# Linear attention of a five-stage kernel: the masked logits become the stationary operand, and the attended values leave TensorE in rows

## The chip, the cores and the metric

The kernel runs on one core of one Trainium2 chip. The metric is the device time of one execution in microseconds, the median of three runs. TensorE (PE in the profile) does the matmuls and transposes, VectorE (DVE), ScalarE (ACT) and GpSimd (POOL) the rest, and SyncE's queue (SP) starts most DMAs. The engines run side by side and wait for one another by semaphores.

## The reference

The program is a small Perceiver of two blocks on x of shape (16, 64, 512): cross-attention, gated attention and a quantised linear layer, then cross-attention, linear attention and a mixture of eight experts, each added to x. The change lies in the second linear attention and at the seam to the mixture behind it. What is computed there:

```
x5  = layernorm(x)                                   # 16 items of 64 rows, 512 features
q   = softmax(x5 @ Wq.T + bq, over features)
k   = softmax(x5 @ Wk.T + bk, over the 64 rows) / sqrt(512)
v   = softmax(x5 @ Wv.T + bv, over the 64 rows)
x   = x + (q @ k.T) @ v                              # item by item
x6  = layernorm(x)
x   = x + sum over experts of gate_e * (relu(x6 @ wi.T + bi + (x6 @ A_e.T) @ B_e.T) @ wo.T + bo)
```

## The kernel before, in words

All 1024 rows of x stand in SBUF as `X[128, 8, 512]`: 8 tiles of 128 rows. A tile holds two items of 64 rows, a "pair", so pair j is tile j. Each stage has one instruction stream for each engine, written out by hand in Python loops; the order of the work is the order of the code, and nothing is scheduled later.

`l1_linear_attention` first projects keys and values into feature-major form (`kT`, `vT`), makes the softmax over rows there, and turns `vT` back into rows `V[:, j, :]`. Then a loop over rounds t works on all pairs, a pair in several steps, each step one or two rounds after the one before:

- `queries_pe(t)`: 12 matmuls for the queries of pair t (TensorE, printed as L288, since all products go through one helper).
- DVE subtracts the minimum (L2312), ACT makes the exponential (L2392), DVE takes the reciprocal and scales (L2322, L2323).
- `turn_queries_pe(t-1)`: 4 transposes (L2187); ACT copies them to `qT` (L2388).
- `attended_pe(t-2)`: 4 products of 128x128, stationary the values of the pair, moving the masked logits `at` (L2208). The result is feature-major, so it has to be turned back.
- `logits_pe(t-1)`: 4 products summed in bank 3 (L2196); DVE multiplies with the block mask into `at` (L2318), so that the two items of a pair don't see each other.
- ACT copies the attended values to `oT` (L2398), `back_pe_of(t-3)` turns them into rows by 4 transposes (L2216), and DVE adds them to `X` (L2327, in the next stage L2687). Behind the sum come the statistics of the next layernorm (L219 to L221), the power on GpSimd (L225) and the normalisation (L229).

An fp32 product of 128x128 appears in the trace as two matmul records, so the 32 products of L2208 are 64 records there; a transpose is one record.

The eight pairs take the rounds t = 0 to 10. On DVE the sums of pairs 6 and 7 stand at the start of the next stage, `l1_mixture`. There TensorE turns the eight normalised tiles (L235: tiles 0 to 3 from the last rounds of the stage before, tiles 4 to 7 behind the first split `xT` of `rows_v`, L305), turns the matrices of LoRA (L2591, L2602, L2604), and makes the gate's logits: 24 products with 8 columns stationary (L288, `gwT`). After that the stage runs over 16 blocks of the hidden layer. `load_half` brings the first two pieces of `wi` into `XT`, where `V` stands until then.

Of the kernel before, what the change touches and what calls it, by code (L numbers as in the profile page):

```python
# [9 lines left out]
ALU = mybir.AluOpType  # L10
# [3 lines left out]
P = 128  # L14
NI, NP, D = 16, 64, 512
NK = 512
C = D // P
KT = NK // P
ROWS = NI * NP
G = ROWS // P  # L20
# [48 lines left out]
def build(nc, a, out):  # L69
# [12 lines left out]
    with ctx:  # L82
# [126 lines left out]
        av = signal("av")  # L209
        back_pe = signal("back_pe")  # L210

# [1852 lines left out]
        def l1_linear_attention():  # L2064
# [7 lines left out]
            o4 = W[:, 0, 1, :].rearrange("p (c n) -> p c n", c=C)  # L2072
            oT = W[:, 5, 0:2, :]
            low = kept["low5"]
# [20 lines left out]
            lg_v = signal("e_lg_v")  # L2095
            at_pe = signal("e_at_pe")
            at_a = signal("e_at_a")

# [7 lines left out]
            def gpsimd():  # L2106
                row_stats_pool(4, PAIRS - 1)
                pool.wait_ge(av.s, av(0))
                p(pool.memset(block[:], 0.0))
                for h in range(2):  # L2110
                    ins = pool.memset(block[h * NP:(h + 1) * NP, h * NP:(h + 1) * NP], 1.0)
                    if h == 0:
                        p(ins)
                ins.then_inc(setup_pool.s, 1)
                pool.wait_ge(setup_pool.s, setup_pool(0))
                for k in range(len(units)):
                    pool.wait_ge(inv_v.s, inv_v(k))
                    seg = segments(k)
                    pool.tensor_tensor(seg, seg, ext[:, k, :].unsqueeze(2).broadcast_to([P, NI // 2, NP]), ALU.mult).then_inc(soft.s, 1)
                for j in range(PAIRS - 2):  # L2120
                    row_stats_pool(5, j)
# [78 lines left out]
            def attended_pe(j):  # L2200
                pe.wait_ge(lg_v.s, lg_v(j))
                pe.wait_ge(vrow_a.s, vrow_a(j if j >= 4 else 3))
                if j >= 2:
                    pe.wait_ge(at_a.s, at_a(j - 2))
                elif j == 0:
                    pe.wait_ge(vrow_a.s, vrow_a(PAIRS - 1))
                for c in range(C):
                    ins = pe.matmul(bank[:, 4 + j % 2, c * P:(c + 1) * P], V[:, j, c * P:(c + 1) * P], at[:], start=True, stop=True)  # L2208
                ins.then_inc(at_pe.s, 1)

            def back_pe_of(j):
                pe.wait_ge(at_a.s, at_a(j))
                if j >= 2:
                    pe.wait_ge(xsum.s, xsum(4 * G + j - 2))
                for c in range(C):
                    ins = pe.transpose(bank[:, 6 + j % 2, c * P:(c + 1) * P], oT[:, j % 2, c * P:(c + 1) * P], ident[:])  # L2216
                ins.then_inc(back_pe.s, 1)

            def tensor():
# [16 lines left out]
                for j in range(4, PAIRS):  # L2236
                    value_rows_pe(j)
                for t in range(1, PAIRS + 3):
                    if t < PAIRS:
                        queries_pe(t)  # L2240
                    if t <= PAIRS:
                        turn_queries_pe(t - 1)
                    if 2 <= t <= PAIRS + 1:
                        attended_pe(t - 2)
                    if t == PAIRS + 1:
                        for g in range(4):
                            transpose_rows(xn6, 5, g, g)
                    if t <= PAIRS:
                        logits_pe(t - 1)
                    if 3 <= t:  # L2250
                        back_pe_of(t - 3)

# [28 lines left out]
            def vector():  # L2281
# [23 lines left out]
                dve.wait_ge(setup_pool.s, setup_pool(0))  # L2305
                for t in range(PAIRS + 3):
                    if t < PAIRS:
# [6 lines left out]
                    if 1 <= t <= PAIRS:  # L2314
                        dve.wait_ge(lg_pe.s, lg_pe(t - 1))
                        if t >= 2:
                            dve.wait_ge(at_pe.s, at_pe(t - 2))
                        dve.tensor_tensor(at[:], bank[:, 3, 0:P], block[:], ALU.mult).then_inc(lg_v.s, 1)  # L2318
                    if t < PAIRS:
# [3 lines left out]
                        dve.tensor_scalar(qj, qj, total, None, ALU.mult).then_inc(probs.s, 1)  # L2323
                    if 3 <= t < PAIRS + 1:
                        j = t - 3
                        dve.wait_ge(back_pe.s, back_pe(j))
                        dve.tensor_tensor(X[:, j, :], X[:, j, :], bank[:, 6 + j % 2, :], ALU.add).then_inc(xsum.s, 1)  # L2327
                        if j:
                            normalise(xn6, 5, j - 1)
                        dve.wait_ge(xsum.s, xsum(4 * G + j))  # L2330
                        row_stats_v(j)
                normalise(xn6, 5, PAIRS - 3)

# [25 lines left out]
            def scalar():  # L2359
# [21 lines left out]
                for j in range(4, PAIRS):  # L2381
                    value_rows_a(j)
                for t in range(PAIRS + 2):
                    if 1 <= t <= PAIRS:
# [4 lines left out]
                    if t < PAIRS:  # L2389
                        qj, lo, total = q[:, t % 2, :], low[:, t % 2, 0:1], low[:, t % 2, 1:2]  # L2390
                        act.wait_ge(lowest.s, lowest(t))
                        act.activation(qj, qj, ACT.Exp, bias=lo, scale=-1.0, accum_out=total).then_inc(expd.s, 1)  # L2392
                    if t >= 2:
                        j = t - 2
                        act.wait_ge(at_pe.s, at_pe(j))
                        if j >= 2:
                            act.wait_ge(back_pe.s, back_pe(j - 2))
                        act.copy(oT[:, j % 2, :], bank[:, 4 + j % 2, :]).then_inc(at_a.s, 1)  # L2398

# [12 lines left out]
        def l1_mixture():  # L2412
# [77 lines left out]
            def sync():  # L2490

                sp.wait_ge(turned.s, turned(5 * G))
                load_half(0)
                load_half(1)
                for q in range(2, 2 * FT // 4):
# [3 lines left out]
            def gpsimd():  # L2499
                pool.wait_ge(score.s, score(PAIRS - 1))  # L2500
                pool.iota(rank[:], pattern=[[-1, E]], base=E, channel_multiplier=0,
                          allow_small_or_imprecise_dtypes=True).then_inc(setup_pool.s, 1)
                for j in (PAIRS - 2, PAIRS - 1):
                    row_stats_pool(5, j)
                pool.wait_ge(setup_pool.s, setup_pool(0))
# [93 lines left out]
            def tensor():  # L2599
                pe.wait_ge(small_in.s, small_in(1))  # L2600
                for c in range(C):
                    ins = pe.transpose(bank[:, 4, c * E:(c + 1) * E], small[0:E, 1, c * P:(c + 1) * P], ident[0:E, 0:E])  # L2602
# [81 lines left out]
            def vector():  # L2684
                for j in (PAIRS - 2, PAIRS - 1):
                    dve.wait_ge(back_pe.s, back_pe(j))
                    dve.tensor_tensor(X[:, j, :], X[:, j, :], bank[:, 6 + j % 2, :], ALU.add).then_inc(xsum.s, 1)  # L2687
                for j in (PAIRS - 2, PAIRS - 1):
                    dve.wait_ge(xsum.s, xsum(4 * G + j))
                    row_stats_v(j)  # L2690
                for g in range(4):
                    rows_v(g)
                dve.wait_ge(wt_a.s, wt_a(0))
                split_v(gwT[:, 1, :, :], gw_src, gwT[:, 0, :, :]).then_inc(wt_v.s, 1)
                for j in (PAIRS - 2, PAIRS - 1):
                    normalise(xn, 5, j)
                for g in range(4, G):
# [210 lines left out]
```

## Time and profile before

| | |
|---|---|
| median of 3 runs | 1278.16 us (1274.45 to 1279.21) |
| profiled execution | 1274.7 us, its span 1273.4 us |
| PE busy | 1222.2 us, 96% of the span |
| DVE, ACT, POOL busy | 730.6, 521.3, 141.2 us |
| chain that ended last | PE 84%, DVE 9%, ACT 4% |
| granted TensorE clock, mean | 0.988 of full speed |
| rounds of the changed stage and the seam | about 965 to 1025 us of the span |

Matmuls are pipelined: a row of the timeline gives the time from the first start to the last (modelled) end, and the next instruction can begin before that end. The chain cuts these overlaps away.

### The profile page before, as it was taken

How to read it: one execution, taken by the hardware profiler on the slowest of the kernel's cores; microseconds unless marked ns; L12 is line 12 of the kernel's file. 1: busy time of each engine (PE TensorE's matmuls, PEld its weight loads, DVE VectorE, ACT ScalarE, POOL GpSimd, SP SyncE). 2: the span in 40 equal slices, each digit the busy share in tenths (PEclk: the TensorE clock that was granted, in tenths of full speed). 3: DMA queues.
4: the chain of work that ended last, by engine and by line, in shares of the span. 5: the costliest groups of instructions: out<-in, count | busy, mean ns of one | idle time of the engine just before them, and what ended most of it. 6: DMA issues, size and time to landing. Idle time of an engine off the chain costs nothing.

```text
span 1273.4 us, 25892 instructions
## 1 busy us (share of the span) xinstructions
PE 1222.2 (96%) x11069; PEld 914.6 (72%) x11069; DVE 730.6 (57%) x1604; ACT 521.3 (41%) x1033; POOL 141.2 (11%) x163
## 2 busy tenths in 40 slices
PE   6999989999979999999999999999899999999999
PEld 4664477865537777777777777777788868888887
DVE  4458386749894555454555555555685756344442
ACT  3234356653122354544454545454454432222321
POOL 2300012055642000000000000000031100000000
PEclk9999999899999999999999999999999899999999
DMA  9659700100204020100010000000400201110100
GB/s 296 249 199 394 286 2 1 66 9 1 99 18 165 1 100 35 34 35 34 35 35 35 35 34 35 34 35 34 85 1 1 75 1 34 33 34 33 66 34 33
DMA packets 49334, 88.23 MB, mean 69 GB/s; under 512 B 19210, under 2 KB 20284, under 8 KB 45124
## 3 DMA queue, kind: packets, MB, share of 16 engines
q1 hardware_dynamic: 48160, 86.01, 19.4%
q8 instruction: 88, 1.44, 0.4%
q10 hardware_dynamic: 1060, 0.56, 0.2%
q14 instruction: 26, 0.21, 0.1%
HBM read 65.59 MB, written 20.97 MB: 68 GB/s over the span
## 4 chain that ended last, share of the span: by engine, by line
PE 84%; DVE 9%; ACT 4%; DMA 1%; issue 1%; POOL 1%; SPq 0%; POOLq 0%; DVEq 0%; ACTq 0%
PE bank L288 58%; PE bank L245 4%; PE bank L1762 3%; PE bank L564 2%; PE bank L1783 2%; PE bank L546 2%; PE bank L1111 1%; PE bank L1132 1%; DVE W L1360 1%; PE bank L235 1%; PE bank L2527 1%; PE bank L491 1%; DVE stats L219 1%; DMA W<-ctx_turned 1%; PE bank L2196 1%
## 5 line engine op out<-in xcount | busy, mean ns | idle before, releaser
L1995 ACT ACTIVATE W<-W,low 128x512 f32<-128x512 f32 x128 | 91.0, 713 | 57.2 <-DVE low L1901 57.2
L1975 ACT ACTIVATE K<-bank,vecT 128x512 f32<-128x512 f32 x64 | 43.8, 689 | 166.2 <-PE bank L288 166.2
L225 POOL TENSOR_TENSOR rstd<-rstd,half_pow 128x1 f32<-128x1 f32 x48 | 31.6, 660 | 697.7 <-DVE rstd L221 697.7
L1874 DVE TENSOR_TENSOR W<-bank,vecT 128x256 f32<-128x256 f32 x16 | 6.8, 424 | 163.6 <-PE bank L1783 163.6
L1901 DVE CUSTOM_DVE_ANT_0 W<-bank,W 128x512 f32<-128x512 f32 x128 | 80.8, 687 | 30.5 <-PE bank L1762 30.5
L288 PE MATMUL bank<-ctxT,Wkv 128*128 128x512 f32 x384 | 93.6, 396 | 0.3 <-DVE ctxT L305 0.3
L288 PE MATMUL bank<-xT,wT 128*128 128x512 f32 x384 | 92.7, 391 | 0.8 <-ACT W L2829 0.5
L288 PE MATMUL bank<-Wq,Wkv 128*128 128x512 f32 x384 | 93.0, 394 | 0.0
L288 PE MATMUL bank<-Wkv,ctxT 128*128 128x512 f32 x384 | 92.9, 394 | 0.0
L288 PE MATMUL bank<-Wkv,Wq 128*128 128x512 f32 x384 | 92.1, 395 | 0.0
L288 PE MATMUL bank<-woT,hR 128*128 128x512 f32 x384 | 91.7, 394 | 0.1
L288 PEld LDWEIGHTS bank<-Wkv,ctxT 128*128 128x128 f32 x384 | 70.8, 188 | 27.1 <-issue 13.0
L288 PEld LDWEIGHTS bank<-Wkv,Wq 128*128 128x128 f32 x384 | 70.8, 188 | 27.2 <-issue 13.0
L288 PEld LDWEIGHTS bank<-xT,wT 128*128 128x128 f32 x384 | 71.8, 188 | 17.3 <-issue 1.3
L288 PEld LDWEIGHTS bank<-ctxT,Wkv 128*128 128x128 f32 x384 | 70.8, 188 | 15.9 <-issue 1.2
L288 PEld LDWEIGHTS bank<-woT,hR 128*128 128x128 f32 x384 | 70.9, 188 | 14.8 <-DVE W_late L2755 0.5
L288 PEld LDWEIGHTS bank<-Wq,Wkv 128*128 128x128 f32 x384 | 70.9, 188 | 14.8
L2002 ACT COPY PT<-bank 128x512 f32<-128x512 f32 x128 | 65.7, 600 | 19.4 <-PE bank L245 19.4
L1909 DVE TENSOR_SCALAR W<-W,total 128x512 f32<-128x512 f32 x128 | 62.3, 487 | 4.6
L2844 ACT ACTIVATE h<-bank,vecT 128x512 f32<-128x512 f32 x32 | 22.1, 690 | 95.2 <-PE bank L288 90.9
L245 PEld LDWEIGHTS bank<-ident,W 32*128 32x128 f32 x2752 | 46.3, 137 | 19.2 <-issue 11.9
L288 PE MATMUL bank<-z,BT 128*128 128x512 f32 x192 | 53.0, 400 | 0.1
(347 smaller groups left out, 2233.1 us busy)
## 6 DMA issues: line engine op xcount, KB each, us to landing
W<-ctx_turned SPq DMA_DIRECT2D x16, 1024.0 KB, 4.7
W<-in_ctx_dram SPq DMA_DIRECT2D x8, 1024.0 KB, 11.0
ctx_turned<-ctxT SPq DMA_DIRECT2D x8, 1024.0 KB, 8.0
ctx_turned<-W SPq DMA_DIRECT2D x8, 1024.0 KB, 6.8
XT<-in_ctx_dram SPq DMA_DIRECT2D x4, 1024.0 KB, 11.3
XT<-in_L_ffn_wi_dram SPq DMA_DIRECT2D x4, 1024.0 KB, 6.3
XT<-in_L_ffn_wo_dram SPq DMA_DIRECT2D x4, 1024.0 KB, 5.0
raw_own<-in_ctx_dram SPq DMA_DIRECT2D x3, 1024.0 KB, 10.8
```

Of the source, the lines that this page charges most:

```text
L225: pool.tensor_tensor(rstd[:, g:g + 1], rstd[:, g:g + 1], half_pow[:], ALU.pow).then_inc(rstd_ok.s, 1)
L245: ins = pe.transpose(bank[:, first + r, to:to + 32], src_of(t, k)[strip, :], ident[strip, strip])
L288: ins = pe.matmul(dst, stationary(x, k), moving(y, k), start=(first and n == 0), stop=(last and n == len(passes) - 1), skip_group_check=True)
L546: ins = pe.matmul(bank[b * NP:(b + 1) * NP, 4, :], q2T[:, c, j * P + b * NP:j * P + (b + 1) * NP], ctxT[j % 2][:, b, c, :], start=(c == 0) ...
L564: ins = pe.matmul(bank[b * NP:(b + 1) * NP, 6, :], pT[:, k, b * NP:(b + 1) * NP], raws[j % 4][:, b, k, :], start=(k == 0), stop=(k == KT - 1))
L1762: ins = pe.matmul(bank[s2 * NP:(s2 + 1) * NP, 4 + r, :], qT[strip, 2 * rnd + s2, i * NP:(i + 1) * NP], K[strip, 2 * rnd + s2, :], start=Tr ...
L1783: ins = pe.matmul(b[32 * r:32 * r + 32, c * NP:(c + 1) * NP], V[:, k, c * P + 32 * r:c * P + 32 * r + 32], PT[:, 4 * (c // 2) + r, k, NP * ...
L1901: dve.tensor_tensor_reduce(out=PR[:, j, :], in0=bank[:, 4 + j % 4, :], in1=mask, scale=1.0, scalar=3.0e38, op0=ALU.add, op1=ALU.min, accum ...
L1909: dve.tensor_scalar(PR[:, j, :], PR[:, j, :], total[:, j:j + 1], None, ALU.mult).then_inc(probs.s, 1)
L1975: act.activation(K[:, m, :], bank[:, n % 4, :], ACT.Identity, bias=pcol("L1_xattn_bk", m)).then_inc(ring_a.s, 1)
L1995: act.activation(PR[:, j, :], PR[:, j, :], ACT.Exp, bias=low[:, j:j + 1], scale=-1.0, accum_out=total[:, j:j + 1]).then_inc(expd.s, 1)
L2002: act.copy(PT[:, 4 * half:4 * half + 4, :, strip].rearrange("p t k n -> p (t k) n"), bank[:, 4 + n % 4, :].rearrange("p (a n) -> p a n", n ...
```

## The change

The product is formed the other way round: `at` (the masked logits, 128x128) is stationary, the values `V[:, j, :]` (128x512) move, and the result of one matmul call is already in rows. The transposes back, ACT's copy to `oT` and their semaphores go. Four banks (4 to 7) are used in turn for the result, instead of two and two. DVE adds pair t-2 in round t (before: t-3), so that the loop has one or two rounds fewer on each engine. At the seam, three of the four transposes of normalised tiles come before the last attended product, only pair 7's sum is left to the next stage on DVE, and the normalisation of pair 6 comes before the statistics of pair 7. The second piece of `wi` now waits for the last attended product, since it lands where `V` is read.

```diff
             def attended_pe(j):
                 pe.wait_ge(lg_v.s, lg_v(j))
                 pe.wait_ge(vrow_a.s, vrow_a(j if j >= 4 else 3))
-                if j >= 2:
-                    pe.wait_ge(at_a.s, at_a(j - 2))
+                if j >= 4:
+                    pe.wait_ge(xsum.s, xsum(4 * G + j - 4))
                 elif j == 0:
                     pe.wait_ge(vrow_a.s, vrow_a(PAIRS - 1))
-                for c in range(C):
-                    ins = pe.matmul(bank[:, 4 + j % 2, c * P:(c + 1) * P], V[:, j, c * P:(c + 1) * P], at[:], start=True, stop=True)
-                ins.then_inc(at_pe.s, 1)
-
-            def back_pe_of(j):
-                pe.wait_ge(at_a.s, at_a(j))
-                if j >= 2:
-                    pe.wait_ge(xsum.s, xsum(4 * G + j - 2))
-                for c in range(C):
-                    ins = pe.transpose(bank[:, 6 + j % 2, c * P:(c + 1) * P], oT[:, j % 2, c * P:(c + 1) * P], ident[:])
-                ins.then_inc(back_pe.s, 1)
+                pe.matmul(bank[:, 4 + j % 4, :], at[:], V[:, j, :], start=True, stop=True).then_inc(rows_out.s, 1)
...
-                for t in range(1, PAIRS + 3):
+                for t in range(1, PAIRS + 2):
                     if t < PAIRS:
                         queries_pe(t)
                     if t <= PAIRS:
                         turn_queries_pe(t - 1)
+                    if t == PAIRS + 1:
+                        for g in range(3):
+                            transpose_rows(xn6, 5, g, g)
                     if 2 <= t <= PAIRS + 1:
                         attended_pe(t - 2)
                     if t == PAIRS + 1:
-                        for g in range(4):
-                            transpose_rows(xn6, 5, g, g)
+                        transpose_rows(xn6, 5, 3, 3)
                     if t <= PAIRS:
                         logits_pe(t - 1)
-                    if 3 <= t:
-                        back_pe_of(t - 3)
...
-                for t in range(PAIRS + 3):
+                for t in range(PAIRS + 1):
...
-                    if 3 <= t < PAIRS + 1:
-                        j = t - 3
-                        dve.wait_ge(back_pe.s, back_pe(j))
-                        dve.tensor_tensor(X[:, j, :], X[:, j, :], bank[:, 6 + j % 2, :], ALU.add).then_inc(xsum.s, 1)
+                    if 2 <= t:
+                        j = t - 2
+                        dve.wait_ge(rows_out.s, rows_out(j))
+                        dve.tensor_tensor(X[:, j, :], X[:, j, :], bank[:, 4 + j % 4, :], ALU.add).then_inc(xsum.s, 1)
                         if j:
                             normalise(xn6, 5, j - 1)
                         dve.wait_ge(xsum.s, xsum(4 * G + j))
                         row_stats_v(j)
-                normalise(xn6, 5, PAIRS - 3)
...
-                    if t >= 2:
-                        j = t - 2
-                        act.wait_ge(at_pe.s, at_pe(j))
-                        if j >= 2:
-                            act.wait_ge(back_pe.s, back_pe(j - 2))
-                        act.copy(oT[:, j % 2, :], bank[:, 4 + j % 2, :]).then_inc(at_a.s, 1)
...
                 load_half(0)
+                sp.wait_ge(rows_out.s, rows_out(PAIRS - 1))
                 load_half(1)
...
             def vector():
-                for j in (PAIRS - 2, PAIRS - 1):
-                    dve.wait_ge(back_pe.s, back_pe(j))
-                    dve.tensor_tensor(X[:, j, :], X[:, j, :], bank[:, 6 + j % 2, :], ALU.add).then_inc(xsum.s, 1)
-                for j in (PAIRS - 2, PAIRS - 1):
-                    dve.wait_ge(xsum.s, xsum(4 * G + j))
-                    row_stats_v(j)
+                dve.wait_ge(rows_out.s, rows_out(PAIRS - 1))
+                dve.tensor_tensor(X[:, PAIRS - 1, :], X[:, PAIRS - 1, :], bank[:, 4 + (PAIRS - 1) % 4, :],
+                                  ALU.add).then_inc(xsum.s, 1)
+                normalise(xn, 5, PAIRS - 2)
+                dve.wait_ge(xsum.s, xsum(4 * G + PAIRS - 1))
+                row_stats_v(PAIRS - 1)
                 for g in range(4):
                     rows_v(g)
...
-                for j in (PAIRS - 2, PAIRS - 1):
-                    normalise(xn, 5, j)
+                normalise(xn, 5, PAIRS - 1)
```

First TensorE in one round, where the names after the arrow are the moving and the stationary operand. Before:

```order
L288 MATMUL bank<-Wkv,xT 128x512 x12
L2187 MATMUL bank<-ident,q 128x128 x4
L2208 MATMUL bank<-at,XT 128x128 x4
L2196 MATMUL bank<-qT,W 128x128 x4
L2216 MATMUL bank<-ident,W 128x128 x4
```

And after (the lines of the file have moved; L2184 is the old L2187, L2204 the attended product, L2193 the logits):

```order
L288 MATMUL bank<-Wkv,xT 128x512 x12
L2184 MATMUL bank<-ident,q 128x128 x4
L2204 MATMUL bank<-XT,at 128x512
L2193 MATMUL bank<-qT,W 128x128 x4
L288 MATMUL bank<-Wkv,xT 128x512 x12
```

The four transposes behind the logits are gone, and the next queries follow the logits at once.

TensorE at the seam, from the last logits on, as a difference (`W` with `ident` are the normalised tiles and the matrices of LoRA):

```order
-L2216 MATMUL bank<-ident,W 128x128 x4
-L2208 MATMUL bank<-at,XT 128x128 x4
-L235 MATMUL bank<-ident,W 128x128 x16
-L2216 MATMUL bank<-ident,W 128x128 x8
-L2602 MATMUL bank<-ident,W 128x8 x4
-L2604 MATMUL bank<-ident,W 128x128 x4
...
+L235 MATMUL bank<-ident,W 128x128 x12
+L2204 MATMUL bank<-XT,at 128x512
+L235 MATMUL bank<-ident,W 128x128 x4
+L2583 MATMUL bank<-ident,W 128x8 x4
+L2585 MATMUL bank<-ident,W 128x128 x4
```

Twelve transposes back (of pairs 5, 6 and 7) are gone, and the last attended product moved behind twelve of the sixteen tile transposes.

DVE from the last masked logits to the first split of the seam. Before:

```order
L2318 TENSOR_TENSOR at5<-bank,block5 128x128 [waits e_at_pe,e_lg_pe]
L2327 TENSOR_TENSOR X<-X,bank 128x512 [waits back_pe]
L229 TENSOR_SCALAR W<-X,mv,rstd 128x512 [waits rstd_ok]
L219 BN_STATS stats<-X 128x6 [waits xsum]
...
L229 TENSOR_SCALAR W<-X,mv,rstd 128x512 [waits rstd_ok]
L2687 TENSOR_TENSOR X<-X,bank 128x512 [waits back_pe] x2
L219 BN_STATS stats<-X 128x6 [waits xsum]
...
L219 BN_STATS stats<-X 128x6 [waits xsum]
...
L305 TENSOR_TENSOR xT6<-bank,xT6 128x4x128 [waits xt_a] x4
```

And after:

```order
L2305 TENSOR_TENSOR at5<-bank,block5 128x128 [waits rows_out,e_lg_pe]
L2314 TENSOR_TENSOR X<-X,bank 128x512 [waits rows_out]
L229 TENSOR_SCALAR W<-X,mv,rstd 128x512 [waits rstd_ok]
L219 BN_STATS stats<-X 128x6 [waits xsum]
...
L2667 TENSOR_TENSOR X<-X,bank 128x512 [waits rows_out]
L229 TENSOR_SCALAR W<-X,mv,rstd 128x512 [waits rstd_ok]
L219 BN_STATS stats<-X 128x6 [waits xsum]
...
L305 TENSOR_TENSOR xT6<-bank,xT6 128x4x128 [waits xt_a] x4
```

Between the last `at` and the first `xT6` DVE had three sums, three sets of statistics and two normalisations; now it has two of each.

## Rows read from the trace of the kernel before

**Rows 1.** The page's first part: busy time and share of each engine.
```profile
PE 1222.2 (96%) x11069; PEld 914.6 (72%) x11069; DVE 730.6 (57%) x1604; ACT 521.3 (41%) x1033; POOL 141.2 (11%) x163
```
**Rows 2.** Waits, 965 to 1025: waiting for releaser, total us, times, longest.
```profile
DVE at L2318 <- PE bank L2196: 11.5, 8, 1.6
DVE q L2312 <- PE bank L288: 5.7, 7, 1.9
```
**Rows 3.** Chain of waits through the rounds: start us, us, what.
```profile
969.96 2.76 PE bank L288 x12
...
974.99 2.77 PE bank L288 x12
...
980.04 0.44 PE bank L2216 x4
...
1001.90 0.02 issue
```
**Rows 4.** Timeline of two rounds: start, us, engine, line, tiles, [idle before].
```profile
967.53 0.60 PE L2187 MATMUL bank<-ident,q 128*128 128x128 f32 x4
...
968.80 1.16 PE L2196 MATMUL bank<-qT,W 128*128 128x128 f32 x8 [0.68 <-ACT qT L2388]
...
985.55 0.29 DVE L2318 TENSOR_TENSOR at<-bank,block 128x128 f32<-128x128 f32 x1 [1.57 <-PE bank L2196]
...
988.34 0.15 DVE L221 TENSOR_SCALAR rstd<-mv 128x1 f32<-128x1 f32 x1
988.53 0.60 PE L2187 MATMUL bank<-ident,q 128*128 128x128 f32 x4
...
988.73 0.69 DVE L2312 CUSTOM_DVE_ANT_0 q<-bank,bq 128x512 f32<-128x512 f32 x1 [0.23 <-PE bank L288]
...
989.17 0.59 ACT L2388 COPY qT<-bank 128x512 f32<-128x512 f32 x1 [3.67 <-PE bank L2187]
...
989.86 1.10 PE L2196 MATMUL bank<-qT,W 128*128 128x128 f32 x8
```
**Rows 5.** Timeline: one attended product that waited for its input (8 records).
```profile
1005.74 1.16 PE L2208 MATMUL bank<-at,XT 128*128 128x128 f32 x8
```
**Rows 6.** Timeline at 267.61: the same shape as the new product.
```profile
267.61 1.12 PE L1088 MATMUL bank<-oT,centring 128*128 128x512 f32 x2
```
**Rows 7.** That source line: durations of one record, ns, min/median/max.
```profile
L1088 PE MATMUL bank<-oT,centring x16: 592/645/697, 267.6 to 337.9; 128*128 128x512 f32 x16
```
**Rows 8.** Chain of waits at the seam.
```profile
1002.87 0.66 PE bank L2187 x4
...
1005.35 0.45 PE bank L2216 x4
...
1013.07 1.97 PE bank L235 x8
...
1024.36 0.02 issue
```
**Rows 9.** Timeline of DVE at the seam.
```profile
1005.83 0.69 DVE L2327 TENSOR_TENSOR X<-X,bank 128x512 f32<-128x512 f32 x1
...
1007.83 0.15 DVE L221 TENSOR_SCALAR rstd<-mv 128x1 f32<-128x1 f32 x1
...
1008.64 0.55 DVE L229 TENSOR_SCALAR W<-X,mv,rstd 128x512 f32<-128x512 f32 x1 [0.66 <-POOL rstd L225]
...
1011.33 0.68 DVE L219 BATCH_NORM_STATS2 stats<-X 128x6 f32<-128x512 f32 x1
...
1012.33 2.47 DVE L305 TENSOR_TENSOR xT<-bank,xT 128x512 fp32r<-128x512 f32 x4
```
**Rows 10.** Stretches at the seam: length, busy us of each engine, granted clock, DMA share, GB/s.
```profile
1005.35:1010.45 5.10, 5.09 (x45) 4.48 (x42) 4.18 (x10) 2.64 (x5) 0.80 (x3) 1.00 0.36 44
1010.45:1013.07 2.62, 0.00 (x1) 0.01 (x1) 2.48 (x8) 0.67 (x2) 1.13 (x3) 0.84 1.01 300
1013.07:1018.10 5.03, 5.03 (x24) 5.03 (x25) 3.94 (x8) 2.81 (x5) 1.36 (x5) 0.50 0.69 269
1018.10:1024.36 6.26, 6.26 (x28) 2.52 (x27) 3.17 (x5) 1.00 (x3) 0.00 (x0) 0.92 0.01 3
```

More of the change, by code:

```diff
@@ L209, in build @@
         av = signal("av")
-        back_pe = signal("back_pe")
+        rows_out = signal("rows_out")
         side_by_side = {}
@@ L2072, in l1_linear_attention @@
             o4 = W[:, 0, 1, :].rearrange("p (c n) -> p c n", c=C)
-            oT = W[:, 5, 0:2, :]
             low = kept["low5"]
@@ L2095, in l1_linear_attention @@
             lg_v = signal("e_lg_v")
-            at_pe = signal("e_at_pe")
-            at_a = signal("e_at_a")
             def sync():
@@ L2119, in gpsimd @@
                     pool.tensor_tensor(seg, seg, ext[:, k, :].unsqueeze(2).broadcast_to([P, NI // 2, NP]), ALU.mult).then_inc(soft.s, 1)
-                for j in range(PAIRS - 2):
+                for j in range(PAIRS - 1):
                     row_stats_pool(5, j)
@@ L2316, in vector @@
                         if t >= 2:
-                            dve.wait_ge(at_pe.s, at_pe(t - 2))
+                            dve.wait_ge(rows_out.s, rows_out(t - 2))
                         dve.tensor_tensor(at[:], bank[:, 3, 0:P], block[:], ALU.mult).then_inc(lg_v.s, 1)
@@ L2382, in scalar @@
                     value_rows_a(j)
-                for t in range(PAIRS + 2):
+                for t in range(PAIRS + 1):
                     if 1 <= t <= PAIRS:
@@ L2502, in gpsimd @@
                           allow_small_or_imprecise_dtypes=True).then_inc(setup_pool.s, 1)
-                for j in (PAIRS - 2, PAIRS - 1):
-                    row_stats_pool(5, j)
+                row_stats_pool(5, PAIRS - 1)
                 pool.wait_ge(setup_pool.s, setup_pool(0))
@@ L2600, in tensor @@
                 pe.wait_ge(small_in.s, small_in(1))
+                pe.wait_ge(xsum.s, xsum(4 * G + PAIRS - 3))
                 for c in range(C):
@@ L2694, in vector @@
                 split_v(gwT[:, 1, :, :], gw_src, gwT[:, 0, :, :]).then_inc(wt_v.s, 1)
-                for j in (PAIRS - 2, PAIRS - 1):
-                    normalise(xn, 5, j)
+                normalise(xn, 5, PAIRS - 1)
                 for g in range(4, G):
```

## Prediction

> **What bounds the kernel now.** I read the page's busy shares first: TensorE is busy for 96% of the span [rows 1], so time is won where TensorE's own work shortens, or where the few stretches in which it waits shorten. Second, the chain of waits through the rounds of the changed stage [rows 3]: from 974.99 on the chain is TensorE alone, piece after piece, and the four transposes back (L2216, 0.44 us) stand on it. Third, the waits of the same stretch [rows 2]: DVE waits for TensorE 11.5 us in all at `at` and 5.7 us at the query minimum. DVE follows, it does not lead. Fourth, the chain at the seam [rows 8] and DVE's timeline there [rows 9]: between 1005.35 and 1013.07 the chain leaves TensorE. The reader is to see that TensorE stands idle for the last 2.6 us of it [rows 10] until DVE has made two sums, two sets of statistics and the first split. Last, the granted clock in the stretches at the seam [rows 10]: it is down to 0.50, the 1.2 GHz level, from 1013.07 to 1018.10.
>
> **The rounds: the transposes back.** A round without them shows in the trace itself: from 969.96 to 974.99, 5.03 us, and from 974.99 to the end of the logits at 980.04, 5.05 us. From there to 1001.90 [rows 3] lie four rounds that each contain four transposes back: 21.86 us, 5.46 each. After the change they should take 5.04 each, since the queries that follow have their bank free. That is 4 x 0.42 = 1.7 us less. The transposes of pair 4 end beside a wait for DVE's scaled query (TensorE's next piece starts at 1002.87 [rows 8], 0.97 us after the logits), so they were hidden and give nothing. Those of pairs 5 to 7 belong to the seam.
>
> **The rounds: the attended product.** It stands between the transposes of the query (L2187) and the logits (L2196), and the logits need ACT's copy of those transposes. In a round with the product the logits start 1.33 us after the transposes (988.53 to 989.86, with the copy ending at 989.76); in the first round, which has no product, they start 1.27 us after (967.53 to 968.80), and there they take 1.16 us instead of 1.10, because nothing was before them to hide the first weight load [rows 4]. Both end 2.43 us after the transposes began. So the product costs nothing today: ACT's copy covers it, and if it becomes shorter nothing is won. The new form isn't in this stage's trace. The same shape elsewhere, two records of 128x512 fp32 behind a wait, took 1.12 us [rows 6]; the old form behind a wait took 1.16 us [rows 5]. That bounds it from below at -0.04. From above, if the two records did not overlap at all, it would be 2 x 0.70 us [rows 7], 0.24 us more than 1.16; in seven rounds and at the seam that is up to 1.9 us more. I take 0, since the row of the same shape is the nearest one.
>
> **The rounds: DVE.** The sum, normalisation and statistics are done by DVE one round sooner, which adds no work to a full round. But the round is shorter. From the masked logits (985.55) to the last statistic (988.49) DVE needs 2.94 us, and the next queries are ready 2.78 us after the logits once the transposes no longer stand between; before, DVE had 0.23 us left there (the wait before 988.73) [rows 4]. So the query minimum starts about 0.2 us late. It feeds ACT's exponential, which anyway stands behind ACT's own copy of `qT`, and the scaled query is not needed until the next round's transposes. DVE's load in a round is 2.94 + 0.69 = 3.6 us of 5.04. I take 0; if the 0.2 us passed through in the six rounds that have both queries and a sum, it would be 1.2 us. ACT's copy to `oT` goes, but ACT waits 3.67 us a round [rows 4], so that gives nothing.
>
> **Last round.** From 1001.90 to 1005.35 (3.45 us) nothing changes: TensorE waits for the scaled query, then transposes, product, logits. It starts 1.7 us sooner.
>
> **The seam up to the first split.** Counted from the end of the last logits (1005.35 before), TensorE's tiles 4 and 5 started at 7.72 us (1013.07) [rows 8]. After: DVE makes `at` (0.33), then sum, normalisation and statistics of pair 6, 2.15 us by the rows of pair 5 (1005.83 to 1007.98 [rows 9]), free at about 2.45. TensorE meanwhile does 12 tile transposes (3 x 0.44 = 1.3) and then the last product (1.1), so pair 7 is also ready at about 2.45: the two meet. Then pair 7's sum 0.69, the normalisation of pair 6 that waits for GpSimd's power (0.66 wait before, here hidden by the sum all but a few hundredths; 0.5), statistics 1.0 (1011.33 to 1012.33), and 0.74 from there to TensorE's start (1012.33 to 1013.07) [rows 8, 9]. The sum is 2.45 + 0.6 + 0.5 + 1.0 + 0.74 = 5.3 us instead of 7.7: 2.4 us less. If the last product took the upper bound, 0.2 of it would go. What could be late next are ACT's copies of tiles 0 to 3, but they begin 0.6 us after the last logits and four take 2.4 us. The weight pieces of `wi` start about 3 us and 1.5 us sooner than TensorE's old schedule; the first is used only behind the gate. The new wait on SP has only `load_half(1)` and later pieces behind it, and it ends 2.5 us after the last logits.
>
> **The seam's clock.** Before, from 1013.07 to 1018.10 TensorE did 24 transposes in 5.03 us at clock 0.50, and the gate's logits behind them ran 6.26 us at 0.92 [rows 10]. At the full clock 24 transposes are 6 x 0.44 = 2.6 us by [rows 3], and the logits 5.8, together 2.9 us less than the 11.3 that they took. TensorE had had no product other than transposes from 1006.9 on [rows 5] before the clock fell, and 2.6 us of idleness. After the change the same stretch is about 6 us instead of 11, with about 1.6 us idle. Whether the dip stays is not decided by any row: the bounds are 0 (it costs the same) and -2.9 (it is gone). I take -1.2, a dip that remains but in less work; the normalisation of pair 6, which the old order left until the first four splits were done, can no longer hold the transposes up.
>
> The Trainium skill ("TensorE: Matmul & The Clock Gate", Part 4: PE-mode transpose) says that transposes don't count as TensorE being busy for the clock. The trace agrees as far as it goes: TensorE was busy 5.03 of 5.03 us with transposes from 1013.07, and the clock stayed at 0.50 [rows 10]. By this rule the change, which puts 12 transposes in a row before the last product and leaves 36 behind it, could keep the dip and even start it sooner.
>
> **Sum.** -1.7 - 2.4 - 1.2 = -5.3 us on an execution of 1274.7 us (span 1273.4, and 1.3 us around it): 1269.4 us. Everything behind the gate's logits hangs on TensorE in the same way as before and just moves. The profiled execution is 3.5 us below the median of the three runs and near the lowest of them; against the median 1278.2 the forecast is 1272.8 us, 0.41% less. A change under 0.5% can hardly be told from none in this kernel, whose three runs lie 0.37% apart.
>
> **Rivals.**
> First, the clock dip goes entirely, as the stretch without products is halved. For it: the last logits and the last product now stand 2.5 us nearer to the gate's logits. Against it: most of that stretch is still transposes and idleness. Then -1.7 - 2.4 - 2.9 = -7.0 us, 1271.2 us.
> Second, what is won comes back: the dip costs as much as before (0) and DVE, which now has no slack at the query minimum, passes 0.2 us on in six rounds (+1.2). For it: 0.23 us of slack is less than the 0.42 us by which the round shortens [rows 4]. Against it: DVE waits 1.57 us for the logits in the same round [rows 4]. Then -1.7 - 2.4 + 1.2 = -2.9 us, 1275.3 us.
> Third, slower: the clock falls before the seam. TensorE's wait for the scaled query in the last round grows from 0.5 to 0.97 us, since the hidden transposes are gone, and the transposes of tiles then come before the last product. If the clock stood at 0.50 from there to the end of the gate's logits, all of TensorE's work in between would double: transposes, product and logits 2.4 us, 16 + 8 tile and LoRA transposes 2.6, the last product 0.9, 24 transposes 2.6 and the gate 5.8, together 14.3 us. Of the added 14.3 about 3 us fall into TensorE's waits. Against the rows of before, -4.1 - 2.9 + 14.3 - 3 = +4.3 us, 1282.5 us. It turns the sign once more than about 10 us (at full clock) of TensorE's work there are at the low level. Against it: from 1005.35 to 1010.45, with 36 transposes and one product, the clock was still 1.00 [rows 10].
>
> **Chances and range.** Forecast 0.55; dip gone 0.22; won and lost 0.16; slower 0.07 (and this one mostly by less than 0.5%). The likeliest case's own range is a gain of 3 to 6.4 us, 1271.8 to 1275.2; single executions spread over 5 us and a median of three by some 2 us either way, so I give 1267.5 to 1277.5. Faster by over 0.5% (6.4 us) is the second case and the edge of the first: 0.27. Within 0.5%: 0.69. Slower: 0.04.
>
> **What would show it.** Right: the chain's rounds of the changed stage 5.03 to 5.08 us; the attended product as two records in about 1.1 us behind the transposes, with the logits still 1.33 us after these; 3.4 us from there to the last logits; TensorE's L235 of tiles 4 and 5 at 5.2 to 5.4 us after the last logits; the gate's logits over 8.5 to 11 us after that. Wrong: rounds over 5.2 us, with a wait of TensorE on DVE or ACT before the transposes or the logits; the split at the seam waiting for ACT; a clock of 0.50 in the rounds themselves.

## The result, and the profile after

The changed kernel takes 1270.9 us (median of 18 executions, 1266.4 to 1277.3) against 1276.9 us of the kernel before (18 executions in the same comparison, 1270.3 to 1282.2). The ratio is 0.9955, with a 95% interval of 0.9941 to 0.9969: about 0.45% faster, and clear of noise. The forecast was 1272.8 us and 0.41%. One execution of the kernel before in a later comparison (1382.1 us) and one of e2 (1737.4 us) ran at a much lower granted clock (0.844 and 0.747) and are left out of all ratios and means below.

The page's first part, which answers to [rows 1]:

```profile
PE 1214.2 (96%) x10989; PEld 902.6 (71%) x10989; DVE 730.6 (58%) x1604; ACT 516.7 (41%) x1025; POOL 141.0 (11%) x163
```

ACT has lost its eight copies (1033 instructions before) and DVE kept all of its own. TensorE has 80 records fewer: 32 transposes back, and 8 products of two records in place of 32 with two.

The waits of the changed stage, against [rows 2]:

```profile
DVE at L2305 <- PE bank L2193: 10.9, 8, 1.6
DVE q L2299 <- PE bank L288: 2.6, 3, 1.9
```

DVE still waits for TensorE at the masked logits. At the query minimum it waited 7 times before and now 3 times: in the rounds that also have a sum, DVE has become the later one there.

The chain of waits through the rounds and over the seam, to set against [rows 3] and [rows 8]:

```profile
968.59 2.74 PE bank L288 x12
...
973.60 2.77 PE bank L288 x12
...
977.67 0.97 PE bank L2193 x8
978.64 2.74 PE bank L288 x12
...
998.75 0.02 issue
...
1002.21 0.02 issue
...
1002.53 0.59 DVE X L2314
...
1005.25 0.55 DVE W L229
...
1006.80 0.61 DVE xT L305
...
1007.46 1.25 PE bank L235 x8
...
1016.10 0.02 issue
```

From 978.64 the queries follow the logits at once. The four rounds to 998.75 take 20.11 us (21.86 before). Last logits to tiles 4 and 5: 1002.21 to 1007.46, 5.25 us (7.72). From there to the end of the gate's logits: 8.64 us (11.29). The stretches of the seam, against [rows 10] (length, busy us of PE, PEld, DVE, ACT, POOL, granted clock, DMA share, GB/s):

```profile
1005.73:1007.46 1.73, 0.01 (x1) 0.01 (x1) 1.66 (x6) 0.67 (x2) 0.57 (x2) 1.00 0.77 253
1007.46:1010.27 2.81, 2.81 (x24) 2.55 (x25) 2.81 (x7) 2.12 (x5) 1.36 (x5) 1.00 0.94 331
1010.27:1016.10 5.83, 5.83 (x29) 2.43 (x28) 3.66 (x7) 1.27 (x4) 0.00 (x0) 1.00 0.15 58
```

TensorE is idle for 1.7 us instead of 2.6, and in this execution the clock does not fall: the 24 transposes take 2.8 us, not 5.0.

One round on its engines, against [rows 4]:

```profile
981.22 0.60 PE L2184 MATMUL bank<-ident,q 128*128 128x128 f32 x4
...
981.59 0.69 DVE L2299 CUSTOM_DVE_ANT_0 q<-bank,bq 128x512 f32<-128x512 f32 x1
...
981.65 1.02 PE L2204 MATMUL bank<-XT,at 128*128 128x512 f32 x2
...
981.85 0.59 ACT L2374 COPY qT<-bank 128x512 f32<-128x512 f32 x1 [3.71 <-PE bank L2184]
...
982.49 0.97 PEld L2193 LDWEIGHTS bank<-qT,W 128*128 128x128 f32 x8 [0.64 <-ACT qT L2374]
982.51 1.14 PE L2193 MATMUL bank<-qT,W 128*128 128x128 f32 x8
```

The weight loads (PEld) of the logits wait 0.64 us for ACT's copy, and the product's two records fill just that time. DVE's minimum has no idle time in front of it.

The two profiled executions differ by 8.2 us of span (1273.4 and 1265.2), which is more than the change gives. 1.4 us of it lie before the first full round (969.96 against 968.59), where both kernels have the same instructions. The rest: rounds 1.75 us, the seam up to tiles 4 and 5 2.47 us, and the stretch from there to the end of the gate's logits 2.65 us, here called the clock's part.

### The profile page after: what moved, and what is told of

Same layout as the page of the kernel before. It is cut to its first block, busy times and chain, and to the rows that moved or that the text cites. A ratio compares the mean times of both kernels' runs of the same rounds, so it can differ in the third digit from the quotient of the medians.

```text
span 1265.2 us, 25713 instructions
## 1 busy us (share of the span) xinstructions
PE 1214.2 (96%) x10989; PEld 902.6 (71%) x10989; DVE 730.6 (58%) x1604; ACT 516.7 (41%) x1025; POOL 141.0 (11%) x163
## 4 chain that ended last, share of the span: by engine, by line
PE 84%; DVE 9%; ACT 4%; issue 1%; DMA 1%; POOL 1%; SPq 0%; POOLq 0%; DVEq 0%; ACTq 0%
PE bank L288 58%; PE bank L245 4%; PE bank L1762 3%; PE bank L1783 2%; PE bank L564 2%; PE bank L546 2%; PE bank L1111 1%; PE bank L1132 1%; DVE W L1360 1%; PE bank L2507 1%; PE bank L235 1%; PE bank L491 1%; DVE stats L219 1%; DMA W<-ctx_turned 1%; PE bank L2193 1%
```

## The experiments

Spans and means below are of executions of each kernel; the kernel before ran in every comparison. Its 44 executions in the comparisons of e1 to e7 have a mean of 1277.3 us, the 23 of the changed kernel (the result and e7) 1270.7 us.

**e1_sums_late.** The new product, with DVE's sums and the seam in the old order (TensorE's tile transposes stand behind the last product again, too):

```diff
-                    if 2 <= t:
-                        j = t - 2
+                    if 3 <= t:
+                        j = t - 3
...
             def vector():
-                dve.wait_ge(rows_out.s, rows_out(PAIRS - 1))
-                dve.tensor_tensor(X[:, PAIRS - 1, :], X[:, PAIRS - 1, :], bank[:, 4 + (PAIRS - 1) % 4, :],
-                                  ALU.add).then_inc(xsum.s, 1)
-                normalise(xn, 5, PAIRS - 2)
-                dve.wait_ge(xsum.s, xsum(4 * G + PAIRS - 1))
-                row_stats_v(PAIRS - 1)
+                for j in (PAIRS - 2, PAIRS - 1):
+                    dve.wait_ge(rows_out.s, rows_out(j))
+                    dve.tensor_tensor(X[:, j, :], X[:, j, :], bank[:, 4 + j % 4, :], ALU.add).then_inc(xsum.s, 1)
+                for j in (PAIRS - 2, PAIRS - 1):
+                    dve.wait_ge(xsum.s, xsum(4 * G + j))
+                    row_stats_v(j)
```

> The changed kernel with the sums and the seam in the old order: DVE adds pair t-3 in round t, the sums of pairs 6 and 7 and both their statistics stand at the start of the next stage, and the four tile transposes come behind the last product. The new product form stays, without transposes back. Theory A (rounds and seam are separate terms): rounds stay at 5.03 to 5.05 us, and tiles 4 and 5 (L235 x8) start 7.4 to 7.6 us after the last logits instead of 5.25, so 2.2 us of the gain go. If the clock dip at the seam comes back with the longer stretch without products, another 1 to 2.7 us go. Rival B (the shorter rounds only work because DVE's sums come sooner, or the reverse): rounds over 5.2 us.

Measured: ratio to the kernel before 0.9985 (0.9966 to 1.0004), so in whole executions it is not told from the kernel before. Chain at the seam (DVE's sums of the last two pairs, then TensorE):

```profile
1009.64 0.59 DVE X L2312
...
1012.91 1.19 DVE X L2668 x2
...
1016.77 1.97 PE bank L235 x8
1018.73 1.62 PE bank L2571 x8
1020.35 0.87 PE bank L235 x8
```

The last logits ended at 1009.32, so the tiles start 7.45 us after them, as theory A said; the rounds stay at 5.04 us. The stretch behind took 10.02 us (to 1026.79): the clock fell in a part of it. The two terms are separate, and the larger one is the order of DVE's work at the seam, since the chain from 1009.35 to TensorE's start runs through DVE's list of work. In whole executions e1 loses more than these 2.2 us: its 12 have a mean of 1275.7 us, 4.9 us above the changed kernel, at a mean granted clock of 0.9850. The kernel before has 0.9851 and the changed kernel 0.9873. So with the old order of the seam the clock was on average as low as before, although in the one profile the dip cost only 1.4 us (10.02 against 8.64).

**e2_idle_transposes.** The changed kernel with transposes that nobody reads where those back had stood:

```diff
                     if t <= PAIRS:
                         logits_pe(t - 1)
+                    if 3 <= t < PAIRS:
+                        if t >= 4:
+                            pe.wait_ge(xsum.s, xsum(4 * G + t - 4))
+                        for c in range(C):
+                            pe.transpose(bank[:, 4 + t % 4, c * P:(c + 1) * P], W[:, 5, 0, c * P:(c + 1) * P], ident[:])
```

> The changed kernel with four transposes of unused data back behind the logits in rounds 3 to 7, where the transposes back were; nobody reads their result. Theory A (the transposes back stood on TensorE's path in four rounds and were hidden in the fifth): rounds that end 3 to 6 take 5.46 us again, the wait for the scaled query in the last round shrinks from 0.97 to 0.53 us, and the time rises by 1.7 us over the changed kernel. Rival B (the rounds got shorter since ACT and DVE had less to do): rounds stay near 5.03 us.

Measured: ratio 0.9965 (0.9946 to 0.9984), mean 1273.1 us (11 executions), 2.4 us over the changed kernel, where 1.7 was expected. The chain:

```profile
978.28 0.44 PE bank L2243 x4
978.72 2.77 PE bank L288 x12
...
983.75 0.44 PE bank L2243 x4
984.19 2.74 PE bank L288 x12
...
1001.11 0.66 PE bank L2184 x4
```

The rounds take 5.47 us again, with nothing but TensorE's own work added. Four of the five groups are on the chain. The fifth, after the logits that end at 1000.15, is not: TensorE's wait for the scaled query became 0.54 us (0.97 without them). Theory A holds; ACT's and DVE's lighter load gave nothing in the rounds.

**e3_product_cut.** The attended product of seven pairs cut to a sixteenth:

```diff
-                pe.matmul(bank[:, 4 + j % 4, :], at[:], V[:, j, :], start=True, stop=True).then_inc(rows_out.s, 1)
+                cols = slice(0, 32) if j < PAIRS - 1 else slice(0, D)
+                pe.matmul(bank[:, 4 + j % 4, cols], at[:], V[:, j, cols], start=True, stop=True).then_inc(rows_out.s, 1)
```

> The changed kernel with the attended product of pairs 0 to 6 cut to 32 of its 512 columns (the other columns of the result are whatever the bank holds, so the output differs); the last pair's product is whole. Theory A (ACT's copy of the turned queries covers the product): the logits still start about 1.3 us behind the transposes, and a round still takes 5.0 us, at most 0.1 us less. Rival B (the product is on the path): 0.8 us less in each of seven rounds, 5 to 6 us in all.

Measured: ratio 0.9949 (0.9927 to 0.9971), the changed kernel's own. TensorE's timeline in one round:

```profile
982.44 0.60 PE L2184 MATMUL bank<-ident,q 128*128 128x128 f32 x4
982.88 0.31 PE L2205 MATMUL bank<-XT,at 128*128 128x32 f32 x2
983.71 1.16 PE L2193 MATMUL bank<-qT,W 128*128 128x128 f32 x8 [0.53 <-ACT qT L2375]
```

The product is almost gone, and the logits start 1.27 us after the transposes and take 1.16 us: the picture of the first round in [rows 4]. The queries started at 974.80, 979.83 and 984.87, so the rounds take 5.03 us. The product is covered by ACT's copy, and its form can give or cost nothing here unless it grows.

**e6_product_in_four.** The same product with `at` stationary, in four calls:

```diff
-                pe.matmul(bank[:, 4 + j % 4, :], at[:], V[:, j, :], start=True, stop=True).then_inc(rows_out.s, 1)
+                for c in range(C):
+                    cols = slice(c * P, (c + 1) * P)
+                    ins = pe.matmul(bank[:, 4 + j % 4, cols], at[:], V[:, j, cols], start=True, stop=True)
+                ins.then_inc(rows_out.s, 1)
```

> The changed kernel with the attended product as four calls of 128 columns (eight records, the masked logits loaded eight times) instead of one of 512. Theory A (the form of the product doesn't matter, since the copy covers it and the records stream alike): rounds 5.03 to 5.06 us, seam within 0.1 us, no change in time. Rival B (the form matters: fewer loads of the stationary operand are part of the gain): rounds 0.03 to 0.1 us longer, up to 0.6 us.

Measured: ratio 0.9951 (0.993 to 0.9972). The chain in two rounds:

```profile
982.47 0.89 PE bank L2206 x8
983.37 0.94 PE bank L2193 x8
984.30 2.76 PE bank L288 x12
...
987.50 0.89 PE bank L2206 x8
988.39 0.94 PE bank L2193 x8
989.34 2.77 PE bank L288 x12
```

The product takes 0.89 us of the chain in four calls and 0.86 in one, the logits behind it 0.94 and 0.97: the 0.03 us only change places, and the round is 5.04 us. Theory A.

**e4_before_filled.** The kernel before, with products in its idle stretch:

```diff
                 ins.then_inc(proj.s, 1)
+                pe.wait_ge(xsum.s, xsum(4 * G + PAIRS - 2))
+                for _ in range(3):
+                    pe.matmul(bank[:, 6, :], ident[:], X[:, 0, :], start=True, stop=True)
                 rows_pe(4)
```

> The kernel before, with three fp32 products of 128x512 that nobody reads (six records, about 2.6 us at full clock) put into TensorE's idle stretch at the seam, behind the sum of pair 6. Theory A (the clock falls at the seam since only transposes and idleness stand there, and that costs up to 2.9 us): clock 1.00 from 1013 on, the 24 transposes and the gate's logits 8.4 to 8.8 us instead of 11.3, and the time 1 to 2.9 us under that of the kernel before on average. Rival B (the dip has another cause, or comes at random): clock 0.50 over those transposes again, no gain or up to 0.5 us more.

**e9_before_again, e10_before_third, e7_after_again, e11_after_third.** No edit; further profiled executions of both kernels.

> The kernel before, profiled once more, for the clock at the seam. If the dip there comes every time: 0.50 in a part of the 24 transposes and the gate's logits, 1.4 to 2.9 us over the 8.4 at full clock. If it is a matter of luck in both kernels: 1.00 in one of the two profiles.

> As e9_before_again, a third profiled execution of the kernel before.

> The changed kernel once more, to see whether the clock at the seam is the same in a second profiled execution. If the dip is gone for good: 1.00 from the last product to the gate's logits, these stretches as before. If it comes in a part of the executions: 0.50 in a part of the 24 transposes or the gate's logits in this one or another of the variants with the same seam.

> A third profiled execution of the changed kernel, for the clock at the seam. The dip was seen in one of its two profiles and in none of the three variants with the same seam; if it comes in about one of five, this one shows 1.00 and 8.6 us from tile 4 to the gate's end.

**e5_after_filled.** As e4, in the changed kernel with two products.

> The changed kernel with two fp32 products of 128x512 that nobody reads in TensorE's idle stretch at the seam (about 1.7 us of idleness, 1.7 us of products). Theory A (in the changed kernel the dip at the seam still comes in a part of the executions): the mean is up to 1 us lower, and the profile shows clock 1.00 at the seam. Rival B (the dip is gone from the changed kernel anyway): no difference, or up to 0.3 us more, as the fill ends late.

All of them in one view: the stretch from the start of tiles 4 and 5 to the end of the gate's logits, with its granted clock behind the busy times. First e9 and e10, of the kernel before (its first profile has 11.29 us at 0.73):

```profile
1015.97:1027.19 11.22, 11.22 (x50) 7.55 (x51) 7.12 (x13) 3.81 (x7) 1.35 (x5) 0.74 0.32 123
```
```profile
1015.63:1026.90 11.27, 11.27 (x50) 7.53 (x51) 7.11 (x13) 3.82 (x7) 1.35 (x5) 0.73 0.32 122
```

e7 and e11, of the changed kernel (its first profile has 8.64 us at 1.00):

```profile
1008.43:1018.41 9.98, 9.98 (x50) 6.59 (x51) 6.57 (x12) 3.60 (x7) 1.36 (x5) 0.84 0.35 125
```
```profile
1012.39:1022.40 10.01, 10.01 (x50) 6.61 (x51) 6.56 (x12) 3.59 (x7) 1.35 (x5) 0.83 0.31 109
```

e4, the kernel before filled, and e5, the changed kernel filled:

```profile
1016.67:1025.77 9.10, 8.79 (x50) 4.96 (x51) 6.93 (x13) 3.51 (x7) 1.36 (x5) 1.00 0.39 151
```
```profile
1012.65:1021.27 8.62, 8.62 (x50) 4.97 (x51) 6.48 (x12) 3.38 (x7) 1.36 (x5) 1.00 0.42 146
```

In the kernel before the dip is there in three profiles of three; the stretch takes 11.26 us on average. With products in the idle stretch (e4) the clock stays up and it takes 9.10 us, so the dip costs 2.2 us there. Of the 0.46 us that still part e4 from the changed kernel's 8.64, 0.31 us is a wait for the normalisation of pair 6 that shows once TensorE is at full speed. e4 fills the idleness and adds products at once; which of the two keeps the clock up was not tested apart. In the changed kernel the dip is there in two profiles of three and costs less, 1.35 us. Counting e2, e3 and e6, whose seam is the same and whose stretch took 8.61 to 8.65 us, it came in two of six. In whole executions e4 is not told from the kernel before (0.9983, 0.9961 to 1.0005; the mean is 2.3 us lower than in the same comparison), and e5 not from the changed kernel (0.9947, 0.9923 to 0.9971; means 1271.4 and 1270.7). So e4's theory A is shown in the trace, not by the times, and e5's stays open: if the fill gains, it is less than could be measured. The expectation of e11, that this one would show 1.00, was wrong. e7 gave a ratio of 0.9942 (0.9923 to 0.996), the result once more.

**e8_gap_used** and **e12_gap_used_sooner.** Can TensorE's 1.7 us of idleness be used? e8, on TensorE (ACT takes tile 6 before the LoRA copies to match):

```diff
-                rows_pe(4)
-                rows_pe(5)
                 pe.wait_ge(lb_in.s, lb_in(E - 1))
                 lora_b_pe(0)
                 lora_b_pe(1)
+                rows_pe(4)
+                rows_pe(5)
                 rows_pe(6)
-                rows_pe(7)
                 pe.wait_ge(xt_v.s, xt_v(3))
                 pe.wait_ge(wt_v.s, wt_v(0))
-                logits_pe(0)
+                product(bank[0:E, 4, :], lambda h, c: gwT[:, h, c, :], lambda h, c: xT[:, h, c, 0:512], 2, last=False)
+                rows_pe(7)
+                product(bank[0:E, 4, :], lambda h, c: gwT[:, h, c + 2, :], lambda h, c: xT[:, h, c + 2, 0:512], 2, first=False)
```

e12 splits the product after one step of three matmuls instead of two steps of six:

```diff
-                product(bank[0:E, 4, :], lambda h, c: gwT[:, h, c, :], lambda h, c: xT[:, h, c, 0:512], 2, last=False)
+                product(bank[0:E, 4, :], lambda h, c: gwT[:, h, c, :], lambda h, c: xT[:, h, c, 0:512], 1, last=False)
                 rows_pe(7)
-                product(bank[0:E, 4, :], lambda h, c: gwT[:, h, c + 2, :], lambda h, c: xT[:, h, c + 2, 0:512], 2, first=False)
+                product(bank[0:E, 4, :], lambda h, c: gwT[:, h, c + 1, :], lambda h, c: xT[:, h, c + 1, 0:512], 3, first=False)
```

> The changed kernel with the seam rearranged: the first eight LoRA transposes go into TensorE's idle 1.7 us before the first split, and the last tile's transposes stand in the middle of the gate's first twelve products instead of ahead of them. Theory A (the seam is now bound by DVE's splits and the last normalisation; work moved under them is free): from the start of tile 4's transposes to the end of the gate's logits 7.8 us instead of 8.6, about 0.8 us less, which the time of whole executions can't show; the clock at the seam stays 1.00, as products come sooner. Rival B (ACT's or DVE's queue is late with the last tile): 8.6 us or more.

> As e8_gap_used, but the last tile's transposes stand behind the first three of the gate's products instead of behind six. In e8 TensorE waited 0.7 us before the second half of the gate's products, for ACT's and DVE's split of the last tile and DVE's split of the LoRA matrix behind it. Theory A (only that was late): no wait there, 8.2 to 8.4 us from tile 4's transposes to the gate's end (the changed kernel: 8.64), and under 0.1% in the whole time. Rival B (DVE's queue of splits sets the end wherever the transposes stand): 8.9 us again.

Measured, e8: 9.00 us from 1014.59 to 1023.59, more than the 8.64 of the changed kernel, ratio 0.9954 (0.9932 to 0.9976). Rival B. TensorE waits 0.70 us before the second twelve of the gate's products, since DVE comes to the last tile only at 1019.21 and to the LoRA matrix `AT` at 1019.82:

```profile
1018.31 1.64 PE L288 MATMUL bank<-xT,gwT 128*8 128x512 f32 x6
...
1019.21 0.69 DVE L305 TENSOR_TENSOR xT<-bank,xT 128x512 fp32r<-128x512 f32 x1 [0.54 <-ACT xT L2773]
1019.82 0.68 DVE L305 TENSOR_TENSOR AT<-bank,AT 128x512 fp32r<-128x512 f32 x1
...
1020.64 2.93 PE L288 MATMUL bank<-xT,gwT 128*8 128x512 f32 x12 [0.70 <-DVE AT L305]
```

e12's chain: 8.38 us, as its theory A said, with no wait left before the second half:

```profile
1013.49 1.85 PE bank L235 x12
...
1016.77 2.08 PE bank L288 x9
...
1018.92 2.95 PE bank L288 x12
```

Its ratio is 0.9932 (0.991 to 0.9954), the lowest of all. It beats the kernel before, but the interval overlaps that of the changed kernel, and the trace explains 0.26 us (0.02%). Whether e12 is faster than the changed kernel stays open.

## Why the prediction was right

- Rounds, -1.7 us: the trace shows -1.75 (21.86 to 20.11), and e2 brings it back by transposes alone. The fifth group was hidden, as said.
- The product, 0: right, and by the reason given (e3, e6). The upper bound of 2 x 0.70 us was never near; one product takes 1.02 us from first start to last end.
- DVE's query minimum about 0.2 us late: the queries were ready at 981.38, the minimum began at 981.59. It was not passed on: rounds take 5.04 us. The second rival falls in both its parts.
- The last round, 3.45 us: 3.46 (998.75 to 1002.21).
- The seam, 5.3 instead of 7.7 us: 5.25, and 7.45 with the old order (e1).
- The seam's clock, -1.2 us inside the bounds of 0 and -2.9: this term was the mis-sized one. It was a guess between two bounds, as no row decided it. That the stretch gained 1.3 us where the dip stayed (e7, e11) is near the guess by luck; what the forecast left out is that in some executions there is no dip. The bound was too wide as well: the 24 transposes and the logits take 8.64 us at full clock, not 8.4. The stretch shortened by 2.65, 1.31 and 1.28 us in the three profiles against 11.29, on average by 1.7; with e2, e3 and e6 counted in, by 2.2 us. The first rival (the dip goes entirely) happened in the execution that was profiled first, but not in two others. Its argument, a shorter stretch without products, is borne out on average and not for each execution: with the old order of the seam (e1) the mean clock is that of the kernel before, with the new order it is higher, and yet the same new seam has a dip in some profiles and none in others. That something in this stretch makes the clock fall is shown by e4 for the kernel before, since there only products were added.
- The third rival, a dip before the seam, did not occur in any of the profiles: the rounds were 5.03 to 5.05 us in every variant without transposes back, the last round 3.45 to 3.47. Where the dip came in the changed kernel (e7, e11) it did begin sooner, 5.1 us behind the last logits instead of 6.9, but still in TensorE's idleness before tiles 4 and 5.

Together, with the clock's part at about 2, -1.75 - 2.47 - 2 = -6.2 us, against the 1277 us of the kernel before 0.49%; the ratio's interval, 0.31 to 0.59%, holds this, and the 5.3 us of the forecast and the 7.0 us of the first rival as well. The times alone can't separate them. Forecast and first rival share the first two terms, which are there in the traces to 0.1 us; what the clock gave lies between the two.

## What to carry to other kernels

When a product can be formed with its operands in exchanged roles so that its result comes out in the layout that is wanted, the transposes back are the gain, not the product's form; look whether the product itself is covered by another engine's copy before counting it. At the seam of two stages, count what one engine does in order between the last input and the first output: taking one sum and one set of statistics out of that queue gave more here than the transposes in four rounds. And compare a term of one or two microseconds in the traces of several executions: a single pair of profiles overstated this change by 2 us.

## What the runs showed of the hardware

- The spread of the times goes with the granted clock. Over 44 executions of the kernel before a straight line through time against mean clock falls by 1.1 us for each 0.001 of clock; over 23 of the changed kernel too. Two such lines of the same slope lie 4.1 us apart, near the 4.2 of rounds and seam (an estimate; at the six levels that both kernels have, the means differ by 2.5 to 5.0 us). The mean clock itself rose from 0.9851 to 0.9873, worth some 2.5 us on that line. This is a second reading of the clock's part, apart from the profiles. Read in the same way, e1 lies 2.3 us above the changed kernel, as its seam says (7.45 against 5.25), and e4 within 0.3 us of the kernel before: what e4 may have gained is in its clock, 0.9877 against 0.9854 in the same comparison. The line doesn't say where in the execution the clock fell; all six profiles of the two kernels also have dips elsewhere, near 250 and 900 us for instance.
- Whether the clock rises while TensorE does transposes alone differs between the profiles. In the kernel before TensorE was busy with transposes for 5.03 of 5.03 us at clock 0.50 [rows 10], and the clock rose only behind them, 0.8 to 1.0 us into the gate's logits (in all three profiles). In the changed kernel, where the dip came, it ended while TensorE still had nothing but transposes, 0.9 us before the first of the gate's logits. This is e7 from the start of tiles 4 and 5 on:

```profile
1008.43:1011.80 3.37, 3.37 (x16) 3.37 (x17) 3.37 (x7) 1.68 (x3) 1.36 (x5) 0.51 0.92 330
1011.80:1012.61 0.81, 0.81 (x11) 0.81 (x9) 0.12 (x1) 0.68 (x3) 0.00 (x0) 1.00 0.45 164
```

  e11 and e1 show the same. So the rule on transposes that the prediction quotes agrees with the rows it had, and not with these: here the measurement decides. Three products of 128x512 in front of the transposes kept the clock at 1.00 (e4); in the first profile of the changed kernel it stayed there without them.
- An fp32 product of 128x512 with 128 columns stationary takes 0.86 us of the chain, four of 128x128 take 0.89.
